# Rotary embedding in the local layers: the query side's cosine product moves from VectorE to GpSimd

## The chip, the cores and the metric

The kernel runs on one core of a Trainium2 chip. The metric is the device time of one execution in microseconds (us), the median of three. On the page of the profile PE is TensorE, DVE is VectorE, ACT is ScalarE, POOL is GpSimd and SP is SyncE, which only issues transfers here.

## What is computed

The reference is a "macaron" block on an input x of 2 sequences of 1,024 tokens with 128 features. Twice, before and after one global attention, it runs a stack of six local layers, so twelve local layers in all. Cut to what matters, each is:

```python
for i in range(6):
    x = attn_layer(shift_tokens(x), Wqkv[i], q_scale[i], k_scale[i], Wo[i]) + x
    x = ffn_layer(shift_tokens(x), ln_g[i], ln_b[i], W1[i], b1[i], W2[i], b2[i]) + x

def attn_layer(x, Wqkv, qs, ksc, Wo):           # 16 heads of 64, window 32
    q, k, v = split(x @ Wqkv)
    q, k = l2norm(q) * qs, l2norm(k) * ksc
    q = q * cos * scale + rotate_half(q) * sin * scale
    k = k * cos / scale + rotate_half(k) * sin / scale
    return local_attention(q, k, v) @ Wo
```

The change concerns the four products in the two rotary lines: q and k each with a cosine and a sine table.

## The kernel before

Tokens are worked on in units of 128; a layer has 16 units, which alternate between the two sequences. For each unit TensorE makes q, k and v in three passes each (lines 492 to 494), ScalarE squares q and k (L694), VectorE sums the squares (L867), finds the inverse square root in eleven small dependent steps (`rsqrt`, L145 to L155) and multiplies q and k by it (L878), which gives `qn`. Then the rotary products: GpSimd makes the sine products of both sides into `by_sin` (L780, two instructions of half a head's width for each side) and the cosine product of the key side into `by_cos` (L784). VectorE makes the cosine product of the query side (L888). TensorE adds the two by transposing both into the same PSUM bank (L450 and L452), queries first, then keys. ScalarE copies the queries out (L648) and the keys out (L655, two copies for each of two parts); TensorE makes the scores (L469).

The softmax of a unit runs one and two steps later: VectorE takes the maximum and subtracts it (`less_top`, L854 and L857), ScalarE takes exponents (L675), VectorE sums, divides and transposes in 32x32 blocks (L813, L817, L823, L833), and ScalarE places the blocks on a diagonal (`diagonal`, L665 to L670, eight copies). TensorE multiplies them with v (`values`, L483 and L484), then with Wo (`output`, L424), and VectorE adds the residual (L845, L847).

All engines run the same software pipeline, written out by hand. In step U of a layer each engine works on unit U for the projections and the norm, on unit U-1 for the rotary transposes and scores, on U-2 for the softmax and on U-3 for the values and the output. Steps 0 to 2 fill the pipeline, a hardware loop of three rounds of four steps runs it, and one step and a written-out end empty it. The order within each engine is fixed by the program, and engines wait for each other by semaphores that count up. The eleven steps of `rsqrt` on VectorE are interleaved with the pieces of the softmax of unit U-2.

In each step GpSimd's queue holds: keep the last 32 keys (`keep`, L762), the low part of the next input (`rest`, L754), and the rotary products of unit U. After the sixteenth unit of a layer that is not the last of its half (ten layers), SyncE loads the next layer's projection weights and scales (L299, L300) into the storage of the squares and of `qn`, once the rotary products of the last unit are made; GpSimd then rounds the weights (L305), makes their low part (L310) and multiplies the rotary tables by the scales (L317). During this the feed-forward part of the layer begins on the other engines: `centre` (L896), `deviation` (small steps and L904), `normal` (L909, L911) and `hidden` (L918) on VectorE, the squares (L718) and the gelu (L737) on ScalarE, and on TensorE the variance (L559) and the products with W1 and W2 (L577, L578, L585).

Of the kernel before, what the change touches and what calls it, by code (L numbers as in the profile page):

```python
# [7 lines left out]
P = 128  # L8
NT = T // P
DEPTH, HEADS, DH, WIN = 6, 16, 64, 32  # L10
# [16 lines left out]
def macaron_program(nc, x_in, wqkv_in, wo_in, w1_in, w2_in, vec_in, scale_in, ma_down_in, ma_heads_in,  # L27
# [4 lines left out]
    with ctx:  # L32
# [3 lines left out]
        def sem(name):  # L36
            return ctx.enter_context(nc.semaphore(name))
# [15 lines left out]
        def bank(b, n=1):  # L53
# [5 lines left out]
        xs_ready, qk_ready, v_ready = sem("xs_ready"), sem("qk_ready"), sem("v_ready")  # L59
        lo_ready, w_hi, w_split = sem("lo_ready"), sem("w_hi"), sem("w_split")  # L60
        sq_ready, qn_ready, cos_ready = sem("sq_ready"), sem("qn_ready"), sem("cos_ready")
        k_cos_ready = sem("k_cos_ready")
        sin_ready, turn_ready = sem("sin_ready"), sem("turn_ready")
        t_ready, t_out, v_out = sem("t_ready"), sem("t_out"), sem("v_out")
        k_kept, s_ready, s_taken, p_ready = sem("k_kept"), sem("s_ready"), sem("s_taken"), sem("p_ready")
# [29 lines left out]
            "tensor": [qk_ready, v_ready, t_ready, s_ready, o_ready, wo_ready, mu_ready, var_ready,  # L95
                       rb_ready, w1_ready, w2_ready],
            "scalar": [xs_ready, sq_ready, v_out, t_out, p_ready, pt_ready, o_out, fsq_ready, gel_ready],
            "vector": [qn_ready, cos_ready, s_taken, block_ready, y_ready, norm_step, soft_step,
                       xc_ready, diag_ready, xn_ready, hid_ready, x_ready, var_step, aff_step],
            "gpsimd": [lo_ready, w_hi, w_split, sin_ready, k_cos_ready, turn_ready, k_kept],  # L100
        }

        def done(unit, per=1, part=0):

            return unit * per + part + 1 + CREDIT
# [124 lines left out]
        def window_half(half, scope):  # L230
# [80 lines left out]

            def tables(eng, layer):

                eng.wait_ge(cos_ready, done(layer * UNITS - 1))
                eng.wait_ge(k_cos_ready, done(layer * UNITS - 1))
                eng.wait_ge(sin_ready, done(layer * UNITS - 1, 2, 1))
                eng.tensor_tensor(turn.rearrange("p t a e -> p t (a e)"),  # L317
                                  rotary[:].rearrange("p t a e -> p t (a e)"),
                                  scales.unsqueeze(1).broadcast_to([P, NT, 4 * DH]),
                                  ALU.mult).then_inc(turn_ready, 1)  # L320
                eng.wait_ge(turn_ready, done(layer))
# [49 lines left out]
            with nc.Block() as block:  # L371


                @block.sync
                def _(sp):
                    def layer(l):
                        U0, C0 = (l + L0) * UNITS, (l + L0) * CHUNKS
                        sp.wait_ge(wo_ready, done(U0 - 1))
                        plain(sp)
                        sp.dma_start(wo, wo_in[bass.ds(l, 1)].rearrange("a p c n -> p (a c) n")).then_inc(w_out, 16)  # L380

                        sp.wait_ge(x_ready, done(C0 - 1))
                        plain(sp)
                        sp.dma_start(w1, w1_in[bass.ds(l, 1)].rearrange("a p n -> p (a n)")).then_inc(w_ffn, 16)
                        sp.dma_start(w2, w2_in[bass.ds(l, 1)].rearrange("a p c n -> p (a c) n")).then_inc(w_ffn, 16)
                        sp.dma_start(vec, vec_in[bass.ds(l, 1)].rearrange("a p n -> p (a n)")).then_inc(w_ffn, 16)

                        def step(i, k, has):

                            U = U0 + 4 * i + k  # L390
                            if has(0):
                                sp.wait_ge(o_ready, done(U - 2))
                                sp.wait_ge(v_out, done(U - 2))
                                plain(sp)
                                sp.dma_start(v_last[k % 2][96:128, :],
                                             V[(k - 2) % 4][96:128, :]).then_inc(kept[k % 2], 16)

                        attention(sp, step)

                    with sp.Fori(0, DEPTH - 1) as l:  # L400
                        layer(l)

                        last = (l + L0) * UNITS + UNITS - 1
                        sp.wait_ge(turn_ready, done(l + L0))
                        plain(sp)
                        sp.wait_ge(sin_ready, done(last, 2, 1))
                        plain(sp)
                        sp.wait_ge(cos_ready, done(last))
                        sp.wait_ge(k_cos_ready, done(last))
                        plain(sp)  # L410
                        load_projections(sp, l + 1)
                    layer(DEPTH - 1)
# [3 lines left out]
                def _(pe):  # L416
                    with pe.Fori(0, DEPTH) as l:
# [10 lines left out]
                        def turned_scores(V0, i, k, v_behind, between=None, middle=None):  # L428
# [2 lines left out]

                            U = V0 + k
                            pe.wait_ge(sin_ready, done(U, 2, 0))
                            pe.wait_ge(cos_ready, done(U))
                            if isinstance(i, int) and i == 0 and k == 0:
                                pe.wait_ge(x_ready, done(C0 - 1))
                            for p in range(4):
                                if p == 1:
                                    pe.wait_ge(o_out, done(U - 2, 2, 1))
                                if p == 2:  # L440
                                    if middle:
                                        middle()
                                    pe.wait_ge(sin_ready, done(U, 2, 1))
                                    pe.wait_ge(k_cos_ready, done(U))
                                if p >= 2:
                                    pe.wait_ge(t_out, done(U, 4, p - 2))
                                for j in range(4):
                                    c = 4 * (p % 2) + j
                                    o = bank(7 - p % 2)[:, P * j:P * j + P]
                                    pe.matmul(o, by_cos[:, p // 2, 2 * c:2 * c + 2, :], ident,  # L450
                                              start=True, stop=False, is_transpose=True)
                                    last = pe.matmul(o, by_sin[:, p // 2, 2 * c:2 * c + 2, :], ident,  # L452
                                                     start=False, stop=True, is_transpose=True)
                                last.then_inc(t_ready, 1)
# [291 lines left out]
                def _(g):  # L746
                    def layer(l):
# [16 lines left out]
                        def step(i, k, has):  # L764
                            U = U0 + 4 * i + k
                            if has(1):
                                keep(U - 1, k - 1)
                            if has(-1):
                                rest(U + 1, k + 1)
                            if has(0):  # L770
                                t = 2 * i + k // 2
                                hd = DH // 2
                                for q in range(2):
                                    g.wait_ge(qn_ready, done(U, 2, q))
                                    g.wait_ge(t_ready, done(U - 1, 4, 2 * q + 1))
                                    plain(g)
                                    for r in range(2):
                                        tab = turn[:, bass.ds(t, 1), 2 + q, hd * r:hd * r + hd].broadcast_to(
                                            [P, HEADS, hd])
                                        last = g.tensor_tensor(by_sin[:, q, :, hd * r:hd * r + hd],  # L780
                                                               qn[:, q, :, hd * (1 - r):hd * (2 - r)], tab, ALU.mult)
                                    last.then_inc(sin_ready, 1)
                                tab = turn[:, bass.ds(t, 1), 1, :].broadcast_to([P, HEADS, DH])
                                g.tensor_tensor(by_cos[:, 1], qn[:, 1], tab, ALU.mult).then_inc(k_cos_ready, 1)  # L784

                        rest(U0, 0)
                        attention(g, step)
# [15 lines left out]
                def _(v):  # L803
                    with v.Fori(0, DEPTH) as l:
# [55 lines left out]
                        def step(i, k, has):  # L860
                            U = U0 + 4 * i + k
                            if has(0):

                                t = 2 * i + k // 2
                                for q in range(2):
                                    v.wait_ge(sq_ready, done(U, 2, q))
                                    last = v.tensor_reduce(ss[:, HEADS * q:HEADS * (q + 1)],  # L867
# [4 lines left out]
                                rsqrt(v, ss, nwt, norm_step, done(U, RSQRT + 1, 0), ALU.max, 1e-24, None, None,  # L872
                                      between=probabilities(U - 2) if has(2) else ())
                                v.wait_ge(sin_ready, done(U - 1, 2, 1))
                                v.wait_ge(k_cos_ready, done(U - 1))
                                v.wait_ge(cos_ready, done(U - 1))
                                for q in range(2):
                                    v.tensor_tensor(qn[:, q], bank(2 * q, 2).rearrange("p (h e) -> p h e", e=DH),  # L878
                                                    nwt[3][:, HEADS * q:HEADS * (q + 1)].unsqueeze(2)
                                                    .broadcast_to([P, HEADS, DH]), ALU.mult).then_inc(qn_ready, 1)  # L880
                                if has(3):
                                    residual(U - 3, i, k - 3)
                                if k == 0:
                                    v.wait_ge(turn_ready, done(l + L0))
                                v.wait_ge(qn_ready, done(U, 2, 1))
                                v.wait_ge(t_ready, done(U - 1, 4, 1))
                                tab = turn[:, bass.ds(t, 1), 0, :].broadcast_to([P, HEADS, DH])
                                v.tensor_tensor(by_cos[:, 0], qn[:, 0], tab, ALU.mult).then_inc(cos_ready, 1)  # L888
                            if has(1):
                                less_top(U - 1)  # L890

# [665 lines left out]
```

## Time and profile before

| | us |
|---|---|
| median of three runs (lowest to highest) | 4704.75 (4704.15 to 4711.61) |
| the profiled execution, its own time | 4695.61 |
| its span | 4693.8 |
| busy TensorE, VectorE | 4058.7, 3754.1 |
| busy ScalarE, GpSimd | 3051.5, 2034.4 |
| mean granted TensorE clock | 0.953 of full |

The span is the time from the first to the last instruction of the profiled execution; 1.8 us of its own time lie around it. Views are: the page, with the busy time of each engine and the costliest groups of instructions; the durations of one line's instructions; stretches with each engine's busy time; and the timeline, where each row has the start in us from the span's start, the duration in us, the engine, the line and the operation, and in square brackets how long the engine was idle before it and whose work ended that.

### The profile page before, as it was taken

To read this page: it belongs to the slowest core of one execution; us is meant where nothing else is said; L and a number is where in the kernel's file an instruction comes from. 1 tells how busy PE (TensorE), PEld (TensorE's weight loads), DVE (VectorE), ACT (ScalarE), POOL (GpSimd) and SP (SyncE) were. 2 spreads that over 40 slices of the span, in tenths; PEclk is the share of its full clock that TensorE was granted. 3 is DMA by queue.
4 is the path that set the end of the run, shared out by engine and by line. 5 is a ranking of instruction groups with operands and counts; after the bars stand their busy time and mean duration, and the time that the engine had idled before them with its cause. 6 is when DMAs were issued, how large, how long until landed. Compare 5 with 4: busy or idle time off the path is not lost. (4 is left out here: it accounts for less than half of the span.)

```text
span 4693.8 us, 116229 instructions
## 1 busy us (share of the span) xinstructions
PE 4058.7 (86%) x42352; PEld 3115.0 (66%) x42352; DVE 3754.1 (80%) x7533; ACT 3051.5 (65%) x4888; POOL 2034.4 (43%) x1420
## 2 busy tenths in 40 slices
PE   5988988989989889938858689899899898898898
PEld 4866857857758768616535478578577587686685
DVE  7988979979979889845335389799799798798897
ACT  5866857848848758612413478488488487586685
POOL 5544536535536545320010155265355365354452
PEclk9999999999999999967968899999999999999999
DMA  1000000000000000040030000000000000000000
GB/s 51 9 24 14 8 31 7 9 29 9 23 14 9 22 17 8 6 95 2 1 81 2 25 17 9 30 8 8 28 9 23 14 9 22 15 9 24 13 8 13
DMA packets 30619, 88.78 MB, mean 19 GB/s; under 512 B 7504, under 2 KB 13648, under 8 KB 28368
## 3 DMA queue, kind: packets, MB, share of 16 engines
q1 hardware_dynamic: 29104, 80.95, 6.4%
q8 instruction: 209, 3.42, 0.3%
q10 hardware_dynamic: 1152, 3.15, 0.3%
q14 instruction: 154, 1.26, 0.1%
HBM read 38.72 MB, written 1.05 MB: 8 GB/s over the span
## 5 line engine op out<-in xcount | busy, mean ns | idle before, releaser
L780 POOL TENSOR_TENSOR pool<-pool 128x512 f32<-128x512 f32 x768 | 1177.1, 1563 | 1147.0 <-DVE pool L878 1147.0
L450 PE MATMUL psum<-squares,pool 128*128 128x128 f32 x3072 | 710.0, 278 | 66.3 <-POOL pool L784 35.6
L452 PE MATMUL psum<-squares,pool 128*128 128x128 f32 x3072 | 700.2, 275 | 0.0
L492 PE MATMUL psum<-wqkv_hi,xs_lo 128*128 128x512 f32 x1152 | 514.0, 446 | 110.4 <-DVE pool L878 45.5
L867 DVE TENSOR_REDUCE pool<-pool 128x16 f32<-128x1024 f32 x384 | 453.4, 1216 | 177.9 <-ACT pool L694 174.6
L483 PE MATMUL psum<-pool 128*64 128x128 f32 x6144 | 539.5, 289 | 61.7 <-ACT pool L670 54.7
L655 ACT COPY pool<-psum 64x512 f32<-64x512 f32 x768 | 447.3, 582 | 215.2 <-PE psum L452 209.9
L450 PEld LDWEIGHTS psum<-squares,pool 128*128 128x128 f32 x3072 | 432.7, 141 | 149.3 <-issue 61.1
L670 ACT COPY pool<-pool 32x512 f32<-32x512 f32 x768 | 486.7, 634 | 9.0
L694 ACT ACTIVATE pool<-psum 128x1024 f32<-128x1024 f32 x384 | 376.5, 1023 | 171.6 <-PE psum L494 167.7
L493 PE MATMUL psum<-wqkv_lo,xs_hi 128*128 128x512 f32 x1152 | 461.7, 401 | 0.0
L494 PE MATMUL psum<-wqkv_hi,xs_hi 128*128 128x512 f32 x1152 | 460.2, 400 | 0.0
L784 POOL TENSOR_TENSOR pool<-pool 128x1024 f32<-128x1024 f32 x192 | 457.7, 2384 | 0.0
L878 DVE TENSOR_TENSOR pool<-psum,pool 128x1024 f32<-128x1024 f32 x384 | 447.7, 1205 | 6.0 <-DVE pool L155 6.0
L424 PE MATMUL psum<-pool 128*128 128x128 f32 x3072 | 391.8, 280 | 62.3 <-ACT pool L655 62.3
L452 PEld LDWEIGHTS psum<-squares,pool 128*128 128x128 f32 x3072 | 434.5, 141 | 15.9 <-issue 0.2
L483 PEld LDWEIGHTS psum<-pool 128*64 128x64 f32 x6144 | 339.2, 136 | 154.5 <-ACT pool L670 81.5
L424 PEld LDWEIGHTS psum<-pool 128*128 128x128 f32 x3072 | 360.2, 191 | 111.5 <-ACT pool L655 99.4
L484 PE MATMUL psum<-pool 128*64 128x32 f32 x6144 | 420.6, 205 | 0.0
L484 PEld LDWEIGHTS psum<-pool 128*64 128x64 f32 x6144 | 417.8, 136 | 0.0
L888 DVE TENSOR_TENSOR pool<-pool 128x1024 f32<-128x1024 f32 x192 | 384.6, 2003 | 10.4 <-DVE pool L878 2.4
L469 PEld LDWEIGHTS psum<-pool 128*32 128x32 f32 x12288 | 324.3, 108 | 90.9 <-issue 76.4
(167 smaller groups left out, 8172.0 us busy)
## 6 DMA issues: line engine op xcount, KB each, us to landing
pool<-pool SPq DMA_DIRECT2D x192, 128.0 KB, 2.3
pool<-in_wqkv SPq DMA_DIRECT2D x12, 1536.0 KB, 6.1
k_st<-turn_st SPq DMA_DIRECT2D x8, 1536.0 KB, 21.4
pool<-in_wo SPq DMA_DIRECT2D x12, 512.0 KB, 3.5
pool<-in_w SPq DMA_DIRECT2D x12, 341.0 KB, 3.0
pool<-in_w SPq DMA_DIRECT2D x12, 192.0 KB, 2.8
rotary<-in_rotary SPq DMA_DIRECT2D x2, 1024.0 KB, 5.1
pool<-in_scale SPq DMA_DIRECT2D x12, 128.0 KB, 6.6
```

What stands on the lines that cost most here:

```text
L424: last = pe.matmul(bank(7)[:, 0:P], wo[:, c, :], oT[:, c, :], start=(c == 0), stop=(c == PAIRS - 1))
L450: pe.matmul(o, by_cos[:, p // 2, 2 * c:2 * c + 2, :], ident, start=True, stop=False, is_transpose=True)
L452: last = pe.matmul(o, by_sin[:, p // 2, 2 * c:2 * c + 2, :], ident, start=False, stop=True, is_transpose=True)
L483: pe.matmul(o, V[k % 4][:, DH * h:DH * h + DH], pT[:, h, :], start=True, stop=False)
L484: last = pe.matmul(o[:, 0:WIN], v_last[k % 2][:, DH * h:DH * h + DH], pT_last[:, h, :], start=False, stop=True)
L492: pe.matmul(o, xs_lo[:, k % 2, :], wqkv_hi[:, c], start=True, stop=False)
L493: pe.matmul(o, xs_hi[:, k % 2, :], wqkv_lo[:, c], start=False, stop=False)
L494: return pe.matmul(o, xs_hi[:, k % 2, :], wqkv_hi[:, c], start=False, stop=True)
L670: last = a.copy(pT[rows, :, rows], turned_P[rows, :, WIN:2 * WIN])
L780: last = g.tensor_tensor(by_sin[:, q, :, hd * r:hd * r + hd], qn[:, q, :, hd * (1 - r):hd * (2 - r)], tab, ALU.mult)
L784: g.tensor_tensor(by_cos[:, 1], qn[:, 1], tab, ALU.mult).then_inc(k_cos_ready, 1)
L867: last = v.tensor_reduce(ss[:, HEADS * q:HEADS * (q + 1)], sq[:, INNER * q:INNER * (q + 1)].rearrange("p (h e) -> p h e", e=DH), AX.X, ALU ...
```

## The change

The cosine product of the query side leaves VectorE and goes to GpSimd, behind the sine product of the same side. GpSimd now makes, in this order, the query sine (two instructions), the query cosine, the key sine (two) and the key cosine. The semaphore `cos_ready` is counted by GpSimd, twice for each unit, and `k_cos_ready` is gone. VectorE loses the product and the three waits before it. TensorE's waits keep their places and name the new counts, and SyncE has one wait and one semaphore increment less before it loads the next projections.

```diff
             def tables(eng, layer):
-                eng.wait_ge(cos_ready, done(layer * UNITS - 1))
-                eng.wait_ge(k_cos_ready, done(layer * UNITS - 1))
+                eng.wait_ge(cos_ready, done(layer * UNITS - 1, 2, 1))
@@ SyncE
                         sp.wait_ge(sin_ready, done(last, 2, 1))
-                        plain(sp)
-                        sp.wait_ge(cos_ready, done(last))
-                        sp.wait_ge(k_cos_ready, done(last))
+                        sp.wait_ge(cos_ready, done(last, 2, 1))
                         plain(sp)
@@ TensorE
                             pe.wait_ge(sin_ready, done(U, 2, 0))
-                            pe.wait_ge(cos_ready, done(U))
+                            pe.wait_ge(cos_ready, done(U, 2, 0))
...
                                     pe.wait_ge(sin_ready, done(U, 2, 1))
-                                    pe.wait_ge(k_cos_ready, done(U))
+                                    pe.wait_ge(cos_ready, done(U, 2, 1))
@@ GpSimd
                                     last.then_inc(sin_ready, 1)
-                                tab = turn[:, bass.ds(t, 1), 1, :].broadcast_to([P, HEADS, DH])
-                                g.tensor_tensor(by_cos[:, 1], qn[:, 1], tab, ALU.mult).then_inc(k_cos_ready, 1)
+                                    tab = turn[:, bass.ds(t, 1), q, :].broadcast_to([P, HEADS, DH])
+                                    g.tensor_tensor(by_cos[:, q], qn[:, q], tab, ALU.mult).then_inc(cos_ready, 1)
@@ VectorE
                                 v.wait_ge(sin_ready, done(U - 1, 2, 1))
-                                v.wait_ge(k_cos_ready, done(U - 1))
-                                v.wait_ge(cos_ready, done(U - 1))
+                                v.wait_ge(cos_ready, done(U - 1, 2, 1))
...
-                                if k == 0:
-                                    v.wait_ge(turn_ready, done(l + L0))
-                                v.wait_ge(qn_ready, done(U, 2, 1))
-                                v.wait_ge(t_ready, done(U - 1, 4, 1))
-                                tab = turn[:, bass.ds(t, 1), 0, :].broadcast_to([P, HEADS, DH])
-                                v.tensor_tensor(by_cos[:, 0], qn[:, 0], tab, ALU.mult).then_inc(cos_ready, 1)
```

## Rows read from the trace of the kernel before

**Rows 1.** The page: busy us (share of the span) xinstructions.
```profile
PE 4058.7 (86%) x42352; PEld 3115.0 (66%) x42352; DVE 3754.1 (80%) x7533; ACT 3051.5 (65%) x4888; POOL 2034.4 (43%) x1420
```

**Rows 2.** Single lines: duration ns min/median/max, first and last start us, forms.
```profile
L780 POOL TENSOR_TENSOR pool<-pool x768: 1296/1318/2395, 52.8 to 4612.5; 128x512 f32<-128x512 f32 x192
...
L784 POOL TENSOR_TENSOR pool<-pool x192: 2335/2386/2412, 58.9 to 4613.7; 128x1024 f32<-128x1024 f32 x192
...
L888 DVE TENSOR_TENSOR pool<-pool x192: 1226/2272/2410, 53.9 to 4609.1; 128x1024 f32<-128x1024 f32 x192
```

**Rows 3.** Stretches: a filling step and a step of the loop, busy by engine.
```profile
707.90:722.64 14.74, 10.84 (x111) 8.78 (x111) 13.59 (x18) 6.75 (x11) 11.20 (x9) 0.88 0.01 2
...
769.02:785.05 16.03, 15.52 (x201) 13.12 (x197) 15.89 (x32) 13.85 (x23) 9.88 (x8) 1.00 0.05 11
```

**Rows 4.** Timeline of TensorE in one step of the loop.
```profile
572.73 0.45 PE L483 MATMUL psum<-pool 128*64 128x128 f32 x4
...
579.08 0.27 PE L450 MATMUL psum<-squares,pool 128*128 128x128 f32 x1
```

**Rows 5.** Timeline of ScalarE in the same step.
```profile
580.15 1.18 ACT L655 COPY pool<-psum 64x512 f32<-64x512 f32 x2 [0.99 <-PE psum L452]
...
583.46 0.63 ACT L665 COPY pool<-pool 32x512 f32<-32x512 f32 x1
...
587.98 0.64 ACT L670 COPY pool<-pool 32x512 f32<-32x512 f32 x1
```

**Rows 6.** Timeline of VectorE in the same step.
```profile
573.68 2.35 DVE L867 TENSOR_REDUCE pool<-pool 128x16 f32<-128x1024 f32 x2 [0.69 <-ACT pool L694]
576.06 0.18 DVE L145 TENSOR_SCALAR pool<-pool 128x32 f32<-128x32 f32 x1
...
580.91 0.44 DVE L833 STREAM_TRANSPOSE pool<-pool 128x256 f32<-128x256 f32 x1
```

**Rows 7.** Timeline of GpSimd in the same step.
```profile
566.82 6.13 POOL L780 TENSOR_TENSOR pool<-pool 128x512 f32<-128x512 f32 x4 [6.19 <-DVE pool L878]
572.88 2.40 POOL L784 TENSOR_TENSOR pool<-pool 128x1024 f32<-128x1024 f32 x1
```

**Rows 8.** Timeline of GpSimd in the second step of a layer.
```profile
708.11 6.11 POOL L780 TENSOR_TENSOR pool<-pool 128x512 f32<-128x512 f32 x4 [4.70 <-DVE pool L878]
714.18 2.33 POOL L784 TENSOR_TENSOR pool<-pool 128x1024 f32<-128x1024 f32 x1
```

**Rows 9.** Timeline of VectorE beside it.
```profile
713.24 1.01 DVE L145 TENSOR_SCALAR pool<-pool 128x32 f32<-128x32 f32 x1
714.29 2.27 DVE L146 TENSOR_SCALAR pool<-pool 128x32 int32<-128x32 int32 x1
...
717.54 0.19 DVE L155 SCALAR_TENSOR_TENSOR pool<-pool 128x32 f32<-128x32 f32 x1
```

**Rows 10.** Timeline of TensorE: its waits in the second and the fourth step.
```profile
716.75 0.32 PE L450 MATMUL psum<-squares,pool 128*128 128x128 f32 x1 [2.98 <-POOL pool L784]
...
735.84 0.50 PE L492 MATMUL psum<-wqkv_hi,xs_lo 128*128 128x512 f32 x1 [1.68 <-DVE pool L878]
```

**Rows 11.** Timeline of GpSimd at a layer's end, then SyncE's queue.
```profile
621.36 2.38 POOL L784 TENSOR_TENSOR pool<-pool 128x1024 f32<-128x1024 f32 x1
...
631.83 2.75 POOL L305 CAST wqkv_hi<-pool 128x3072 fp32r<-128x3072 f32 x1 [7.52 <-DMA pool<-in_scale]
...
640.35 4.72 POOL L317 TENSOR_TENSOR pool<-rotary,pool 128x2048 f32<-128x2048 f32 x1
...
624.93 0.34 SPq L299 DMA_DIRECT2D pool<-in_wqkv  x1
```

**Rows 12.** Timeline of VectorE and ScalarE at the same layer's end.
```profile
624.22 1.43 DVE L823 TENSOR_TENSOR pool<-pool 128x256 f32<-128x256 f32 x4
...
642.18 4.17 DVE L823 TENSOR_TENSOR pool<-pool 128x256 f32<-128x256 f32 x4
...
648.42 0.63 ACT L718 ACTIVATE pool<-pool 128x512 f32<-128x512 f32 x1 [8.55 <-DVE pool L896]
```

More of the change, by code:

```diff
@@ L61, in macaron_program @@
         sq_ready, qn_ready, cos_ready = sem("sq_ready"), sem("qn_ready"), sem("cos_ready")
-        k_cos_ready = sem("k_cos_ready")
         sin_ready, turn_ready = sem("sin_ready"), sem("turn_ready")
@@ L97, in macaron_program @@
             "scalar": [xs_ready, sq_ready, v_out, t_out, p_ready, pt_ready, o_out, fsq_ready, gel_ready],
-            "vector": [qn_ready, cos_ready, s_taken, block_ready, y_ready, norm_step, soft_step,
+            "vector": [qn_ready, s_taken, block_ready, y_ready, norm_step, soft_step,
                        xc_ready, diag_ready, xn_ready, hid_ready, x_ready, var_step, aff_step],
-            "gpsimd": [lo_ready, w_hi, w_split, sin_ready, k_cos_ready, turn_ready, k_kept],
+            "gpsimd": [lo_ready, w_hi, w_split, sin_ready, cos_ready, turn_ready, k_kept],
         }
@@ L862, in step @@
                             if has(0):
-                                t = 2 * i + k // 2
                                 for q in range(2):
```

## The prediction

> **What bounds the kernel now.** I read the page first: TensorE is busy for 86% of the span and VectorE for 80% [rows 1]. These are averages over filling, loop and feed-forward, so I took stretches next. In a step of the loop, which lasts 16.0 us, TensorE is busy 15.5 and VectorE 15.9; GpSimd is busy 9.9 [rows 3]. By busy time alone VectorE looks like the limit, and the change takes its most suspicious instruction away: L888 has a median of 2.27 us where its shortest is 1.23 [rows 2].
>
> So I followed one step by the timelines. TensorE begins the values at 572.73 and reaches the key transposes at 579.08 [rows 4]; ScalarE copies the first keys out from 580.15, after a wait on TensorE, and then does v, the other keys and eight diagonal copies from 583.46 to 587.98 + 0.64 = 588.62 [rows 5]. The next values need those copies. From 572.73 to 588.73 (0.11 for the signal, as 572.73 had) is 16.0 us: this circle of TensorE and ScalarE is as long as the step. VectorE waits 0.69 us for ScalarE's squares in the same step [rows 6]. So its full bar is work beside the circle, and L888 is in no chain that sets the step.
>
> **Removed from VectorE.** 192 instructions of 2.27 us are 436 us of VectorE's time. On the path of the loop they are worth nothing, because ScalarE's squares don't come earlier: VectorE would only wait longer than 0.69. In the filling steps TensorE does wait for VectorE (1.68 us before the fourth projection, [rows 10]), but that norm's chain starts from squares that L888 doesn't hold up by more than about 0.1. I take 0; were it 0.1, that is 1 us in twelve layers.
>
> **Added to GpSimd.** One product of the shape of L784, 2.39 us, for each unit. Some comes back: of its four L780 one is held while VectorE runs L888 (1.32 us median, 2.40 at most, [rows 2]; four took 6.13, [rows 7]). Six instructions without that are 4 x 1.32 + 2 x 2.39 = 10.05, less 5 overlaps of 0.05 in the records, 9.8 us. Before, from the first to the end of L784, they took 572.88 + 2.40 - 566.82 = 8.5 [rows 7]. The key cosine so ends 1.3 us later. The query side is complete at 2.6 + 2.4 = 4.9 us, and the values that precede its transposes only start at 572.73 - 566.82 = 5.9. The key transposes start 579.08 - 566.82 = 12.3 after GpSimd's start: 2.5 us of cover over 9.8. Uncovered, it would cost what is beyond.
>
> **What GpSimd's longer run does to VectorE.** In the second step of a layer GpSimd is at work from 708.11 [rows 8], and VectorE's small steps beside it, 0.18 us when free [rows 6], take 1.01 and 2.27 [rows 9]. The 2.27 ends at 716.56, where L784 ends (714.18 + 2.33 = 716.51). So an instruction of VectorE that needs what GpSimd holds waits for the end of GpSimd's current one, and one gets in at each boundary; L867 isn't touched. The Trainium skill ("SBUF — State Buffer", Who interferes with whom) says it as a rule: two SBUF inputs or a two-port mode on VectorE and a reading GpSimd instruction shut each other out for a whole instruction, and a reduce never contends; the trace agrees, and by it the move puts more of GpSimd's time in the way of the small steps.
>
> In the loop L145 comes 576.06 - 566.82 = 9.2 us after GpSimd's start, when only `keep` and `rest` are left. After the change it meets the key cosine, which runs from 7.45 to 9.8, is held to 9.8, and L146 meets `keep` or `rest`. That is 0.4 to 0.7 us, and the norm, so GpSimd's next start, comes later by it. But ScalarE's squares keep their time, so L145 meets GpSimd still earlier in its run, and the lateness S grows. When S passes 9.2 - 7.45 = 1.8, L145 gets in before the key cosine; L146 then waits for its end, S + 9.8, where it ended at 10.1 before: S no longer grows. I take S = 1.9. What is late next are the transposes L833: they end at 581.35 [rows 6], and the diagonal copies start at 583.46 [rows 5], 2.1 us of cover. So the step stays at 16.0 us, just. Bounds: S = 0 if the phases let VectorE through, 2.5 if the cover is used up.
>
> **The filling steps.** In the second step TensorE waits 2.98 us for the key cosine [rows 10], so 1.3 us more go straight on. Beside it L145 and L146 are held by the two key sines, L153 by the key cosine to 717.85, L154 by `keep` and L155 by `rest` to some 718.9, where L155 was free at 717.54 [rows 9]: the norm of the second unit is 1.2 to 1.4 us late. In the third step the squares are 1.3 late, L145 arrives where the last sine ends (GpSimd's start at 721.9 + 7.4 = 729.3): 1.4 late if it gets in, 2.5 if not. This reaches TensorE, which already waits there [rows 10]. R = 1.9, between 1.3 and 2.5.
>
> **The end of a layer.** Here the loss is handed on. SyncE starts the next weights at 624.93, 1.2 us after the last key cosine (621.36 + 2.38 = 623.74); GpSimd gets them at 631.83 and ends L317 at 640.35 + 4.72 = 645.07 [rows 11]. VectorE's four L823, 1.43 us when free, take 4.17 from 642.18, to 1.3 us after L317's end; ScalarE has waited 8.55 us for what follows them [rows 12]. So each us by which the rotary products of the sixteenth unit end later goes whole into the layer. They end 1.3 + R + S = 5.1 later. SyncE takes back some of its 1.2 us (I take 0.6, between 0 and 0.9), and the longer chain meets L911 and the first L823 in places where GpSimd waits for them (0.5, between 0 and 1.0). 5.1 - 0.6 + 0.5 = 5.0 us in each of ten layers. The two layers that load nothing lose R and about 0.8 at the last unit's key transposes, 2.7 each. Sum: 10 x 5.0 + 2 x 2.7 = 55 us on 4695.6 of the profiled execution, 4751. The median of the runs stands 9 us above that execution: 4760.
>
> Whether the product should be on GpSimd at all: L784 takes 2.39 us and the same shape on VectorE undisturbed 1.23 [rows 2]. The Trainium skill ("GPSIMD Engine Reference", the table of elementwise measurements) has 1.96 times for a two-input add, and the trace agrees with 1.95; by that rule alone 192 x 1.16 = 223 us would be lost on a serial chain, but most of it here lies beside other work.
>
> **Rivals.**
> Only the exposed parts (S near 0, L145 slips through): 12 x 1.3 in the second steps, and 1.3 + 1.3 - 0.9 = 1.7 for ten layer ends in place of 1.3: about 20 us, up to 30 with R = 1.9; 4725 to 4735. For it speaks that already before, L145 was let in without loss in the loop; against, that 9.2 lies inside the key cosine.
> The circle of GpSimd and VectorE becomes the step's limit: from GpSimd's start 9.8 to the end of the key cosine, then L145 and the rest of the norm, 6.8 (576.06 to the next start, one step after 566.82), is 16.6 where ScalarE's circle has 16.0. It decides if L145 is always held to the end. Less the part that gets in early it would be 16.2 to 16.4; 0.2 to 0.4 x some 11 steps x 12 layers add 26 to 53 us: 4786 to 4813.
> No change: the 1.3 us are hidden and SyncE's slack takes the rest. The wait of 2.98 us in each filling speaks against it; 4700 to 4714.
> Faster: VectorE is the limit after all, at 15.9 of 16.0. It decides if the 0.69 us wait is an echo of VectorE's own lateness, a step before. Then the next limit is TensorE's 15.5: 0.5 x 11 x 12 = 66 us less, plus the filling's 16: 4655. The circle of ScalarE, complete without VectorE, speaks against it.
>
> **Numbers.** A measurement of this kernel tells 0.2% (9.4 us) from no change. Forecast with S between 1 and 2.2: 0.60; exposed parts only 0.16; GpSimd's circle 0.12; no change 0.07; faster 0.05. Slower 0.88, same 0.07, faster 0.05. The forecast's own bounds: R = 1.3, S = 1 and 0.9 taken back give 2.7 x 10 + 4 = 31, so 4736; R = 2.5, S = 2.2 and no relief 7.0 x 10 + 7 = 77, so 4782. For eight in ten I go from 4724 to 4794, into both neighbours.
>
> **What would show it.** Right: six GpSimd instructions in 9.8 us; loop steps still 16.0; L145 or L146 held in them by 1 to 2 us, L833 ending nearly 2 us later against the step and VectorE idle for longer before L867 or `less_top`; the wait of L450 in the second step 4.3 us; L317 and L718 about 5 us later in ten layers. Wrong: loop steps of 16.2 or more with ScalarE waiting for L833 before L665, or steps under 16.0 (VectorE was the limit), or weights landing at their old place in the layer.

## The result and the profile after

The changed kernel takes 4743.68 us (median of four runs, 4736.81 to 4749.95) against 4704.45; the ratio is 1.0095 (1.008 to 1.011). It is slower, by 39 us between the medians and some 45 by the ratio, where 55 were forecast. At the same mean clock, 0.951, the changed kernel took 4736.81 us and the kernel before 4697.29 to 4705.49 in seven executions. The profiled execution took 4749.95 us with a span of 4747.8, 54.0 more than before.

The page first; it answers to [rows 1], and its second part to the lines of [rows 2]:

```profile
PE 4081.2 (86%) x42352; PEld 3135.6 (66%) x42352; DVE 3699.9 (78%) x7341; ACT 3051.4 (64%) x4888; POOL 2293.0 (48%) x1612
...
L776 POOL TENSOR_TENSOR pool<-pool 128x512 f32<-128x512 f32 x768 | 997.6, 1322 | 981.6 <-DVE pool L872 972.4
L780 POOL TENSOR_TENSOR pool<-pool 128x1024 f32<-128x1024 f32 x384 | 917.2, 2388 | 0.0
```

VectorE lost 192 instructions that had taken 2.0 us each on average, 385 us in all, but its busy time fell by 54 us only. GpSimd's sine instructions (L780 before, L776 now) are no longer held: their mean is 1.32 us, the median of before. Most of the rest has gone into VectorE's small steps, L145 above all. Their durations, minimum, median and maximum in ns (before, L144 was line 145, and its median 182; L145 was line 146, and its median 172):

```profile
L144 DVE TENSOR_SCALAR pool<-pool x192: 180/248/2474, 49.5 to 4654.5; 128x32 f32<-128x32 f32 x192
```
```profile
L145 DVE TENSOR_SCALAR pool<-pool x192: 165/1809/2268, 49.7 to 4655.2; 128x32 int32<-128x32 int32 x192
```

One step of the loop on three engines, which answers to [rows 5], [rows 6] and [rows 7]:

```profile
511.77 2.60 POOL L776 TENSOR_TENSOR pool<-pool 128x512 f32<-128x512 f32 x2 [5.23 <-DVE pool L872]
514.33 2.40 POOL L780 TENSOR_TENSOR pool<-pool 128x1024 f32<-128x1024 f32 x1
516.67 2.61 POOL L776 TENSOR_TENSOR pool<-pool 128x512 f32<-128x512 f32 x2
519.20 2.42 POOL L780 TENSOR_TENSOR pool<-pool 128x1024 f32<-128x1024 f32 x1
...
516.71 2.35 DVE L862 TENSOR_REDUCE pool<-pool 128x16 f32<-128x1024 f32 x2 [1.17 <-ACT pool L690]
519.10 0.23 DVE L144 TENSOR_SCALAR pool<-pool 128x32 f32<-128x32 f32 x1
519.84 1.82 DVE L145 TENSOR_SCALAR pool<-pool 128x32 int32<-128x32 int32 x1
525.88 0.43 DVE L829 STREAM_TRANSPOSE pool<-pool 128x256 f32<-128x256 f32 x1
...
526.49 0.63 ACT L661 COPY pool<-pool 32x512 f32<-32x512 f32 x1
```

GpSimd's run takes 519.20 + 2.42 - 511.77 = 9.85 us (forecast 9.8). L144 gets in at the boundary before the key cosine, L145 waits for the cosine's end at 521.6, and the transposes end at 526.31, 0.18 us before ScalarE's first diagonal copy; before, there were 2.1. The step is still 16.02 us. Against ScalarE's squares GpSimd starts 3.9 us ahead (511.77, squares at 515.66) where it was 5.8 ahead (566.82, squares at 572.62): S = 1.9, as forecast.

The cover isn't enough every time. Once or so in a layer L144 comes just after the boundary:

```profile
535.12 2.45 DVE L144 TENSOR_SCALAR pool<-pool 128x32 f32<-128x32 f32 x1
...
542.96 0.63 ACT L661 COPY pool<-pool 32x512 f32<-32x512 f32 x1 [0.46 <-DVE pool L829]
```

It missed the change of instructions at 535.13, was held for the whole cosine, and ScalarE waited 0.46 us for VectorE. Such a step lasts 16.5.

The filling steps on TensorE, which answer to [rows 10]:

```profile
723.18 0.32 PE L446 MATMUL psum<-squares,pool 128*128 128x128 f32 x1 [2.34 <-POOL pool L780]
728.02 0.32 PE L446 MATMUL psum<-squares,pool 128*128 128x128 f32 x1 [1.46 <-POOL pool L780]
741.72 0.32 PE L446 MATMUL psum<-squares,pool 128*128 128x128 f32 x1 [2.91 <-POOL pool L780]
747.34 0.50 PE L488 MATMUL psum<-wqkv_hi,xs_lo 128*128 128x512 f32 x1 [0.98 <-DVE pool L872]
```

The first unit's keys are transposed 728.02 - 718.02 = 10.0 us after GpSimd's first start, before 8.6. The wait for them is only 1.46 us, before 2.98, because TensorE now waits for the queries first: 2.34 us, before 0.92. The second unit's keys now wait for the key cosine too.

The layer's end, which answers to [rows 11] and [rows 12]:

```profile
634.35 0.34 SPq L298 DMA_DIRECT2D pool<-in_wqkv  x1
...
641.32 2.75 POOL L304 CAST wqkv_hi<-pool 128x3072 fp32r<-128x3072 f32 x1 [6.44 <-DMA pool<-in_scale]
644.25 5.62 POOL L309 TENSOR_TENSOR wqkv_lo<-pool,wqkv_hi 128x3072 fp32r<-128x3072 f32 x1 [0.18 <-POOL wqkv_hi L304]
649.83 4.71 POOL L315 TENSOR_TENSOR pool<-rotary,pool 128x2048 f32<-128x2048 f32 x1
...
630.96 4.52 DVE L819 TENSOR_TENSOR pool<-pool 128x256 f32<-128x256 f32 x4
...
639.38 0.87 DVE L892 TENSOR_SCALAR pool<-squares,pool 128x128 f32<-128x128 f32 x4
...
644.48 5.67 DVE L899 TENSOR_SCALAR pool<-pool 128x512 f32<-128x512 f32 x1
651.66 4.16 DVE L819 TENSOR_TENSOR pool<-pool 128x256 f32<-128x256 f32 x4
...
657.89 0.63 ACT L714 ACTIVATE pool<-pool 128x512 f32<-128x512 f32 x1 [10.73 <-DVE pool L884]
```

The last key cosine ends at 634.10 and the load starts 0.25 us later (before 1.2). From GpSimd's start on the sixteenth unit (624.15; before 615.29) to ScalarE's L714 it is 33.7 us, before 33.1. The L819 of the unit before the last, from 630.96, takes 4.52 us, where L823 took 1.43 [rows 12]. From one weight cast to the next, the layers of the first half last 4.7 us more than before (1329.57 - 1310.93 over four), those of the second half 3.6 (1338.72 - 1324.45 over four).

### The profile page after: what moved, and what is told of

Read it like the earlier page. It is cut to its first block and busy times, and to the rows that moved or that the text cites. A ratio compares the mean times of both kernels' runs of the same rounds, so it can differ in the third digit from the quotient of the medians.

```text
span 4747.8 us, 115838 instructions
## 1 busy us (share of the span) xinstructions
PE 4081.2 (86%) x42352; PEld 3135.6 (66%) x42352; DVE 3699.9 (78%) x7341; ACT 3051.4 (64%) x4888; POOL 2293.0 (48%) x1612
## 5 line engine op out<-in xcount | busy, mean ns | idle before, releaser
L776 POOL TENSOR_TENSOR pool<-pool 128x512 f32<-128x512 f32 x768 | 997.6, 1322 | 981.6 <-DVE pool L872 972.4
L780 POOL TENSOR_TENSOR pool<-pool 128x1024 f32<-128x1024 f32 x384 | 917.2, 2388 | 0.0
L446 PE MATMUL psum<-squares,pool 128*128 128x128 f32 x3072 | 720.0, 280 | 95.8 <-POOL pool L780 73.9
L448 PE MATMUL psum<-squares,pool 128*128 128x128 f32 x3072 | 709.3, 277 | 0.0
L488 PE MATMUL psum<-wqkv_hi,xs_lo 128*128 128x512 f32 x1152 | 517.8, 449 | 98.0 <-POOL xs_lo L750 44.0
L448 PEld LDWEIGHTS psum<-squares,pool 128*128 128x128 f32 x3072 | 438.4, 143 | 11.3
L819 DVE TENSOR_TENSOR pool<-pool 128x256 f32<-128x256 f32 x768 | 396.8, 524 | 0.8
L750 POOL TENSOR_TENSOR xs_lo<-pool,xs_hi 128x128 fp32r<-128x128 f32 x192 | 80.6, 420 | 633.4 <-ACT xs_hi L636 633.4
```

Of the source, the lines that this page charges most:

```text
L446: pe.matmul(o, by_cos[:, p // 2, 2 * c:2 * c + 2, :], ident, start=True, stop=False, is_transpose=True)
L488: pe.matmul(o, xs_lo[:, k % 2, :], wqkv_hi[:, c], start=True, stop=False)
L780: g.tensor_tensor(by_cos[:, q], qn[:, q], tab, ALU.mult).then_inc(cos_ready, 1)
```

## The experiments

Ratios are to the kernel before, timed beside each. Diffs are against it unless another is named.

| | us | ratio (95%) |
|---|---|---|
| no query cosine | 4688.85 | 0.9974 (0.9962 to 0.9986) |
| spare product before the keys | 5022.41 | 1.0678 (1.0651 to 1.0705) |
| spare product after the keys | 5016.42 | 1.0673 (1.0645 to 1.0700) |
| spare memsets after the keys | 4738.61 | 1.0083 (1.0061 to 1.0105) |
| changed kernel, weight work late | 4644.25 | 0.9875 (0.9855 to 0.9894) |
| kernel before, weight work late | 4617.84 | 0.9811 (0.9793 to 0.9829) |
| both cosines on VectorE | 4961.10 | 1.0546 (1.0524 to 1.0568) |
| weight work late, key cosine of the filling on VectorE | 4631.28 | 0.9849 (0.9831 to 0.9868) |
| change in the filling only | 4738.45 | 1.0082 (1.0069 to 1.0096) |
| change in the loop only | 4727.95 | 1.0056 (1.0043 to 1.0070) |

**No query cosine.** The product is made by nobody; its buffer is zeroed once, so the queries carry the sine part alone.

```diff
-                                tab = turn[:, bass.ds(t, 1), 0, :].broadcast_to([P, HEADS, DH])
-                                v.tensor_tensor(by_cos[:, 0], qn[:, 0], tab, ALU.mult).then_inc(cos_ready, 1)
+                                v.sem_inc(cos_ready, 1)
```

> The kernel before with the query side's cosine product left out altogether (its buffer is zeroed once, so queries carry the sine part only). Theory (the loop's circle is TensorE and ScalarE, GpSimd's run only holds VectorE's small steps): loop steps stay at 16.0 us, VectorE waits about 3 us a step for ScalarE; GpSimd's run shortens from 8.5 to 7.6 us, so the fillings and the ten layer ends gain about 0.9 us each: 20 us less, 4670 to 4700. Rival (VectorE is the loop's limit): each loop step falls toward TensorE's 15.5 us, 66 us less or more, 4640 or below.

0.26% faster, 12 us where I expected 20, and inside my range. Busy us in 40 us of the loop (PE, PEld, DVE, ACT, POOL, then the granted clock):

```profile
560.00:600.00 40.00, 38.58 (x493) 32.94 (x495) 32.74 (x83) 33.81 (x54) 19.29 (x16) 1.00 0.03 7
```

VectorE is idle for 18% of it and the steps are still 16.0 us. VectorE's work was not what set the loop of the kernel before.

**A spare product on GpSimd, ahead of the key cosine or behind it.** Both leave the query cosine on VectorE. The first delays the keys by 2.35 us; the second leaves them where they were, but the kept keys (`keep`) and the low part of the next input (`rest`), which stand behind it in the queue, come later.

```diff
+                                g.tensor_tensor(spare, qn[:, 1], tab, ALU.mult)
                                 g.tensor_tensor(by_cos[:, 1], qn[:, 1], tab, ALU.mult).then_inc(k_cos_ready, 1)
```
```diff
                                 g.tensor_tensor(by_cos[:, 1], qn[:, 1], tab, ALU.mult).then_inc(k_cos_ready, 1)
+                                g.wait_ge(spare_ready, done(U - 1))
+                                plain(g)
+                                g.tensor_tensor(spare, rotary[:, 0:4].rearrange("p t a e -> p (t a) e"),
+                                                rotary[:, 4:8].rearrange("p t a e -> p (t a) e"),
+                                                ALU.mult).then_inc(spare_ready, 1)
```

> The kernel before, where GpSimd makes one more product of 128x1024 (into a spare buffer) ahead of the key cosine; VectorE keeps the query cosine. Theory: GpSimd's run is 8.5 + 2.35 = 10.8 us where the changed kernel has 9.9, so every loss of the change comes larger: TensorE waits 5.3 us in the second step, VectorE's small steps are held past the 2.1 us of cover and loop steps grow to 16.3 to 16.7: 4790 to 4840. Rival (only what reaches TensorE late costs: 2.35 us in twelve fillings and ten layer ends): 4755 to 4760, loop steps 16.0.

> The kernel before with one more product of 128x1024 on GpSimd, from a table that nobody writes into a spare buffer, behind the key cosine's count, so that no operand of another engine is made later by it; GpSimd is only busy for 2.4 us longer. Theory (a reading instruction of GpSimd holds VectorE's small steps): L145 and L146 meet the spare product, the norm and with it the next GpSimd run come later, loop steps stay at 16.0 or grow to 16.4: 4730 to 4800. Rival (the loss is the late keys, not the holding): 4700 to 4712.

Both are 6.7% to 6.8% slower, with steps of 17.0 to 18.0 us. That they are alike rules out the rival that late keys are their cost. Nor is it the late `keep`: ScalarE waits for it once in 100 us of the loop here (1.4 us), and three times (3.6 us) with the memsets below, which cost far less. But both are far over my 4840 and 4800. The loop of the second one, the same columns and then two of its VectorE rows:

```profile
560.00:600.00 40.00, 35.39 (x452) 29.36 (x440) 39.62 (x69) 32.17 (x52) 26.51 (x18) 1.00 0.03 7
```
```profile
545.12 2.40 DVE L894 TENSOR_TENSOR pool<-pool 128x1024 f32<-128x1024 f32 x1
...
552.32 2.35 DVE L145 TENSOR_SCALAR pool<-pool 128x32 f32<-128x32 f32 x1
```

VectorE is busy, or held, for 99% and is now the limit. GpSimd's queue here is as full as in the changed kernel, four sines and two products, though not in the same order, and one sine is still held (10.8 us for 9.85); what differs most is that VectorE keeps its product (L894, 2.40 us with its hold). So VectorE's relief, worth nothing in the kernel before, pays for the holds in the changed one: without it the same queue costs 6.7% in place of 0.95%.

**Memsets in place of the product.** GpSimd's queue is longer by 2.9 us with the gaps, but nothing is read.

```diff
                                 g.tensor_tensor(by_cos[:, 1], qn[:, 1], tab, ALU.mult).then_inc(k_cos_ready, 1)
+                                for n in range(3):
+                                    g.wait_ge(spare_ready, done(U, 3, n - 1))
+                                    plain(g)
+                                    g.memset(spare, 0.0).then_inc(spare_ready, 1)
```

> As the spare product behind the keys, but GpSimd's extra 2.4 us are three memsets of 900 columns into a spare buffer, which read nothing. Theory (what holds VectorE's two-input steps is GpSimd's reading; boundaries every 0.8 us let the others in): L153 to L155 run free beside the memsets and at most L145 and L146 are held for under 0.8 us each: 4700 to 4730. Rival (any instruction of GpSimd holds any small step of VectorE): as with the spare product, less what the finer boundaries give, 4725 to 4790.

0.8% slower in place of 6.7%: a little over my range, and inside the rival's. So the time doesn't decide between them; the rows do. One step:

```profile
536.85 0.86 POOL L789 MEMSET pool<- 128x900 f32 x1
537.86 0.89 POOL L789 MEMSET pool<- 128x900 f32 x1 [0.15 <-POOL pool L789]
538.90 0.85 POOL L789 MEMSET pool<- 128x900 f32 x1 [0.15 <-POOL pool L789]
539.71 0.63 POOL L763 COPY pool<-pool 128x512 f32<-128x512 f32 x1
...
536.92 0.83 DVE L145 TENSOR_SCALAR pool<-pool 128x32 f32<-128x32 f32 x1
538.47 0.18 DVE L153 TENSOR_TENSOR pool<-pool 128x32 f32<-128x32 f32 x1
538.88 0.43 DVE L828 TENSOR_TENSOR pool<-pool 128x256 f32<-128x256 f32 x1
539.76 0.85 DVE L828 TENSOR_TENSOR pool<-pool 128x256 f32<-128x256 f32 x1
```

The tensor_scalar L145 is held to the end of the first memset. The two-input L153 and the first L828 run free inside the second and third memset, and the third L828 is held by the copy, which reads. This is the rule of the Trainium skill ("SBUF — State Buffer", Who interferes with whom) in both its parts: a VectorE instruction with two SBUF inputs contends only with a GpSimd instruction that reads, one in a two-port mode with any; the trace agrees, 0.18 and 0.43 us beside memsets, 0.83 and 0.85 where held, though no row shows in which mode L145 runs. How much of the difference between 6.7% and 0.8% comes from reading and how much from the shorter instructions isn't shown: no run has one long memset.

**The weight work late.** On GpSimd, at a layer's end, in the kernel before and in the changed one.

```diff
+                        g.wait_ge(block_ready, done((l + L0) * UNITS + UNITS - 1))
+                        plain(g)
                         round_weights(g.tensor_copy, l + L0 + 1)
+                        g.wait_ge(xn_ready, done((l + L0) * CHUNKS + CHUNKS - 1))
                         rest_of_weights(g, l + L0 + 1)
```

> The changed kernel, where GpSimd at a layer's end rounds the next weights only when VectorE has turned the last unit's probabilities, and makes their low part and the tables only when the last chunk's xn is ready. Theory (at the layer's end GpSimd's weight work holds L823, L904 and L911 on VectorE, and that hands the lateness on): nothing on VectorE is held there, each of ten layer ends saves 5 us or more: 50 us off the changed kernel, 4680 to 4705. Rival (the layer end is bound elsewhere): within 10 us of the changed kernel's 4744.

> The same delay of the weight work in the kernel before. Theory: the holds there are 2.9 us at L823 and 1.8 to 4.8 at L904 and L911, of which 3 to 6 us lie on the path, in ten layers: 4645 to 4675. The changed kernel with the same delay stays above it by the lateness of the filling alone, R = 1.9 and 0.8 for the last unit's keys, 2.7 x 12 = 32 us, where the two kernels as they are differ by 40 to 54. Rival (weight work is off the path): 4704, and the difference stays at 40 or more.

The kernel before becomes 1.9% faster, 80 us, and is the fastest of all: 4617.84, below my range. From GpSimd's sixteenth run to the next layer's first, each of the ten layers is shorter by 7.0 us in the first half and by 10.2 in the second, where I expected 3 to 6. The holds of L904 (2.5 us), L911 (1.8) and L823 (2.7) add up to 7.0. That all of them lay on the path isn't shown, since the clock changed as well: between the sixteenth run and the next projection it was 0.96 before and is 1.00 now, and that projection, at 2.4 GHz in the first half before, now runs in part at 1.2 (11.3 us to the first rotary run for 9.7). Two of the steps in the kernel before, and then two of the steps that were held, free now:

```profile
631.29 3.37 DVE L904 TENSOR_SCALAR pool<-squares,pool 128x128 f32<-128x128 f32 x4
...
638.31 2.37 DVE L911 TENSOR_SCALAR pool<-pool 128x512 f32<-128x512 f32 x1
```

```profile
629.34 0.55 DVE L914 TENSOR_SCALAR pool<-pool 128x512 f32<-128x512 f32 x1
...
631.44 1.43 DVE L826 TENSOR_TENSOR pool<-pool 128x256 f32<-128x256 f32 x4
```

The changed kernel gains 99 us, twice what I expected, and comes to 4644.25. Between the two stay 26 us by the medians and 30 by the ratios (32 forecast), where the kernels as they are stand 39 and 45 apart. In the two profiled executions, 29 us apart, the stretch from a layer's first rotary run to its sixteenth is 3.8 us longer in each of twelve layers, 46 us; the ten layer ends give back 7, and the stretch with the global attention 8, at a clock of 0.82 for 0.80. So the filling and the loop hold the cost, and the layer ends add nothing once the weight work is out of the way. That the missing 13 to 15 us went through the weight work is likely, not shown: the 95% intervals nearly cover it.

**Both cosines on VectorE.**

```diff
-                                tab = turn[:, bass.ds(t, 1), 1, :].broadcast_to([P, HEADS, DH])
-                                g.tensor_tensor(by_cos[:, 1], qn[:, 1], tab, ALU.mult).then_inc(k_cos_ready, 1)
@@ VectorE, behind the query cosine
+                                v.wait_ge(t_ready, done(U - 1, 4, 3))
+                                tab = turn[:, bass.ds(t, 1), 1, :].broadcast_to([P, HEADS, DH])
+                                v.tensor_tensor(by_cos[:, 1], qn[:, 1], tab, ALU.mult).then_inc(k_cos_ready, 1)
```

> The kernel before with the key cosine on VectorE too, behind the query cosine: the move of the change made in the other direction. Theory: GpSimd's run is only the four sines, about 7 us with two holds; VectorE, busy 15.9 of 16.0 us with 1.0 of it held, gets 1.2 to 2.3 more and becomes the loop's limit, steps of 16.6 to 17.2, while the filling gains up to 1 us: 4780 to 4860. Rival (what VectorE loses comes back, since its small steps are no longer held): steps of 16.0 and a gain of 1 to 2 us a layer, 4680 to 4705.

5.5% slower, with steps of 17.5 us, and more than expected. VectorE is at 39.62 of 40 us here too. Of the three divisions the one of the kernel before is the best: VectorE has 0.7 us to spare in a step, and a product costs 1.2 to 2.4.

**The filling's key cosine on VectorE,** on top of the late weight work.

```diff
@@ GpSimd
+                                if not (isinstance(i, int) and i == 0):
...
                                     g.tensor_tensor(by_cos[:, 1], qn[:, 1], tab, ALU.mult).then_inc(k_cos_ready, 1)
@@ VectorE, behind the query cosine
+                                if isinstance(i, int) and i == 0:
+                                    v.wait_ge(t_ready, done(U - 1, 4, 3))
...
+                                    v.tensor_tensor(by_cos[:, 1], qn[:, 1], tab, ALU.mult).then_inc(k_cos_ready, 1)
```

> The kernel before with the weight work delayed as in the runs beside it, and in the three filling steps of each layer alone the key cosine on VectorE, behind the query cosine. Theory (in the filling TensorE waits for GpSimd's key cosine, 2.98 us in the second step): the keys are ready 1 us earlier there and VectorE's next norm is held less: 1 to 2 us in twelve layers off its sibling with delayed weights, 4630 to 4665. Rival (the norm chain of VectorE sets the filling, and 1.3 us more on it costs as much): no gain over the sibling.

The rival holds: the time is inside my range, but 13 us slower than its sibling, which I had put too high. GpSimd's start on the second unit follows the first 1.1 us sooner (11.6 for 12.7), but the third and the fourth follow 0.7 and 0.8 later.

**The change in one part of a layer only.** The same product is moved by a condition on the step; this is the filling, and the loop has the condition with "not". VectorE's product has the opposite condition in each.

```diff
+                                    if q == 0 and isinstance(i, int) and i == 0:
...
+                                        g.tensor_tensor(by_cos[:, 0], qn[:, 0], tab, ALU.mult).then_inc(cos_ready, 1)
```

> The change in the three filling steps of each layer only; in the loop and the last step the query cosine stays on VectorE. Theory: the units of the filling come 1.2 to 1.9 us late and TensorE with them, and that stays to the layer's end: 12 x 1.6 = 19 us, 0.3% to 0.5% slower. Rival (the loop wins the filling's lateness back, as the first loop steps of the kernel before are 15.5 us): no change, within 0.1%.

> The change in the loop and the last step only; in the three filling steps the query cosine stays on VectorE. Theory: loop steps at 16.0 us, VectorE late by 1.9 us against ScalarE, which costs 1.5 to 2.5 us at each of ten layer ends: 15 to 27 us, 0.3% to 0.6% slower, and with the filling's part it makes up the whole change. Rival (lateness under the cover is free): no change, and the filling alone makes the whole 0.9%.

Each is slower, 38 and 26 us; the rivals, that the one or the other is free, are out. But the filling costs twice what I expected, and the two don't add up to the whole (64 for some 45). From GpSimd's first start to its sixteenth in a layer they do better: 234.7 us before, 238.3 in the changed kernel, 236.7 and 236.9 in these, means over twelve layers; 2.0 and 2.1 more make 4.1, for 3.5. Much of what doesn't fit lies ahead of the first start. Two stretches from the first projection of the third layer, in the kernel before and with the change in the filling only:

```profile
698.00:702.00 4.00, 3.61 (x16) 3.02 (x17) 0.79 (x1) 1.61 (x2) 0.24 (x1) 1.00 0.72 204
```
```profile
703.50:708.00 4.50, 4.20 (x10) 3.33 (x11) 0.09 (x1) 1.02 (x1) 0.09 (x1) 0.50 0.63 183
```

The granted clock is 1.00 (2.4 GHz) in the one and 0.50 (1.2 GHz) in the other, after the same 2.68 us of waiting by TensorE, and the layer's first rotary run starts 12.2 us after the projection's first matmul instead of 9.7. Over all layers of the profiled executions this way from the first matmul to the first rotary run is 8 and 11 us longer in these two than before, and 4 in the changed kernel. In the profiled executions the mean clock was 0.953 before, 0.945 and 0.943 in these two, and 0.947 in the changed kernel. So differences of 10 to 20 us between such kernels are in part differences of clock, and these two runs tell the sign and the order of the parts, not their exact shares.

## Why the prediction was right, and where it was off

**What bounds the loop:** right. The circle of TensorE and ScalarE stays at 16.0 us with the product (before), without any product, and with it on GpSimd (medians of GpSimd's starts 15.9, 16.0 and 16.0).

**VectorE's relief at 0:** right for the kernel before (without the product the loop's steps stay at 16.0 us, and the 0.26% come in the filling, where GpSimd's starts follow each other 0.7 to 1.0 us faster), and wrong as a statement about the changed one. I counted the 2.1 us of cover before the diagonal copies and left out that VectorE, freed of 2.3 us, had room to be held in. The spare products showed it. The 436 us that I took for the product were its median times 192; it had taken 385, which changed nothing in a term of 0.

**GpSimd's run, 9.8 us:** measured 9.85. The keys 1.3 us later: 1.4.

**The holds and S = 1.9:** measured 1.9, by the mechanism given (L144 in at the boundary, L145 held to the end of the cosine). The cover is used up but for 0.2 us, and now and then it fails by 0.5: of the rival of the circle of GpSimd and VectorE so much is true. How near it was the spare products show: where VectorE keeps its product beside the same queue, it is busy or held all the time, and a step takes 17.0 to 18.0 us.

**The filling, R = 1.9:** the fourth projection's squares came 1.6 us later against GpSimd's first start (33.4 for 31.8). I had not seen that the second unit's keys wait too (2.91 us). Nor did the wait for the keys in the second step grow to 4.3 us, which I had named as a sign of being right: it is 1.46. In the filling there is no work ahead of the query transposes that covers the query cosine, so the wait for the queries grew by 1.4 us, and the keys follow them.

**The end of a layer:** the mis-sized term. 5.0 us for each of ten layers were forecast. By GpSimd's starts, from one layer's first rotary run to the next's, it is 4.9 in the first half and 3.5 in the second. In three parts, each the mean of five layers:

| us more than before | forecast | first half | second half |
|---|---|---|---|
| first to sixteenth rotary run (R + S) | 3.8 | 3.2 | 3.6 |
| from there to the next layer's first projection matmul (L492, now L488) | 1.2 | 0.5 | 0.5 |
| from there to the first rotary run | 0 | 1.2 | -0.5 |

So the end of a layer costs 0.5 us where I had 1.2. SyncE took back 0.95 of its 1.2 us, not 0.6, and of the further holds that I put at 0.5 some came and some went: the first L823 (now L819) is held for 4.52 us in place of 1.43 and L911 (now L899) for 5.67 in place of 2.37, while L904 is free because the weights come later.

The last row is a term that I didn't have, the granted clock. The first 5 us of the fourth layer's first projection, in the kernel before and in the changed one:

```profile
1026.02:1031.02 5.00, 4.36 (x18) 3.29 (x18) 2.12 (x2) 2.96 (x5) 0.38 (x1) 1.00 0.61 167
```
```profile
1039.96:1044.96 5.00, 5.00 (x15) 3.96 (x16) 1.22 (x1) 1.38 (x2) 0.00 (x0) 0.66 0.52 161
```

In the profiled execution of the kernel before, TensorE has the full 2.4 GHz in this stretch in layers two to six, and the first rotary run comes after 9.7 us. In the changed kernel it has that in the third layer only; in the other four a part of the stretch is at 1.2 GHz, and the run comes after 11.1 to 11.4 us. In the second half both kernels are slowed there, the kernel before more (11.1 to 12.1 us for 11.0 to 11.1). That accounts for the difference between the halves. Why the transfer of the weights takes longer there in both kernels (16.9 to 18.3 us from GpSimd's start to the cast, before, where the first half has 16.3 to 16.5) I didn't find.

**The size of the whole:** the profiled execution was 54 us over the one of before, the medians 39 and the ratio 45. That 54 lies so near the 55 is luck. The ten layers that load weights make 42 of it, where 50 were forecast; the last layer of the first half, with the global attention behind it, makes 8 where 2.7 were, and the last layer of all 2.7, as forecast; 1 lies before the first rotary run. The clock in the stretches after the first projection matmul of each layer makes 4 of the 54, and where in the global attention its 3 us arise I didn't follow. The four runs stand in two pairs, 4737 and 4738 at a clock of 0.951 and 0.949, 4749 and 4750 at 0.943 and 0.947; the spread of the clock is in the numbers of this kernel whatever is changed.

## What to carry to other kernels

Before moving a product to GpSimd, look at what VectorE does while GpSimd works: beside GpSimd instructions that read, small two-input and tensor_scalar steps passed only one at a time here, at the ends of GpSimd's instructions (0.18 us became 1.82 or 2.45), so a dependent chain of them is drawn out over GpSimd's run. The time that VectorE is idle, not its busy share, says how much of that it can take. And long GpSimd instructions that nobody needs soon (here 13 us of next weights) belong where VectorE has no such steps: two waits on GpSimd were worth 1.9%, twice what the whole change cost. And before dividing a small difference into parts, compare the granted clock of the same stretch in both kernels, layer by layer.

## What the hardware did that I had not expected

The granted clock at the start of a layer was 2.4 GHz in one kernel and 1.2 GHz in another after the same wait of 2.68 us; matmuls of 128x512 followed each other by 0.23 us in the one and 0.43 in the other, and 2.5 us of the layer hang on it. Within the changed kernel it stayed at 2.4 GHz after a wait of 3.16 us in the third layer and fell in the fourth after one of 2.96, so the length of the wait alone doesn't decide it. And the price of holding is a cliff: 1.0 us more of GpSimd in a step (10.8 for 9.85) together with 2.3 us more on VectorE made a step 1.6 us longer (17.6 us for 16.0).
